# Layer boundaries of a graph network reordered on TensorE, a count scale applied at eviction, twelve tiles taken in row halves

## The chip, the cores and the metric

One core of one Trainium2 chip runs the whole program. The metric is the device time of one execution in microseconds (us). A kernel's time is the median of several executions without the profiler; the profile describes one further execution.

## What is computed

```python
# x: 6250 nodes x 128; src, dst: 200000 edges, sorted by dst; edge_weight per edge
z = x
for l in range(3):                                   # gated layers
    m   = z @ weight[l]
    agg = segment_sum(m[src] * edge_weight[:, None], dst)
    z   = gru_cell(agg, z, w_ih, w_hh, b_ih, b_hh)   # r, z gates: sigmoid; n: tanh; blend
x = layernorm(x + z)
y = x
for W, b in ((W0, b0), (W1, b1), (W2, b2)):          # count layers
    y = relu((y + segment_sum(y[src], dst)) @ W.T + b)
out = layernorm(x + y)
```

## The kernel before, in words

The nodes are padded to 6272, which is 49 tiles of 128. `xT` holds the features across the partitions and the nodes along the free dimension. The edge list is turned once into dense matrices in DRAM: `adj_w` (float32, sums of edge weights) and `adj_h` (float16, edge counts; the identity for the node's own term is part of it). A layer is then a dense product: for each of 14 groups of 448 target nodes, TensorE (PE) adds up 49 matmuls, one for each source tile, with the tile of `Y` (the layer's products, node-major) as the weights and a slab of the streamed matrix as the moving operand.

The program has four stages.

1. **Build, fused with the first gated layer.** 28 spans of 224 nodes. PE makes the matrix of a span out of one-hot operands (line 934, matmuls over 64 rows), and between the batches adds the 49 tiles of the span before (`add_tiles`, line 941). The last span has nothing left to build: its tiles 0 to 12, the gates of span 26, its tiles 13 to 48 and the gates of span 27 (`fused_gates`, lines 954 to 957) stand alone.
2. **Second gated layer**, `gru_layers(1, 1)`: `node_major` (line 719) makes the 49 products of the new layer, in chunks of four tiles that alternate between PSUM banks 6 and 7; DVE copies each chunk into `Y` (line 1300). Then `aggregate` (line 730) and `gates` (lines 740 to 743) for 14 groups, the gates of a group standing behind the aggregation of the next one.
3. **Third gated layer**, `last_gru_layer`: the same, with the sum with x, the statistics of the layer norm (`flip_sums`, line 819, and `statistics`) and, at its end, the products of the first count layer (`first_messages`, line 837), which ACT and DVE split into a high and a low float16 part (`first_highs`, line 1122; `first_lows`, line 1406).
4. **Three count layers**: `halves_of_group` (line 870) adds 49 tiles x 2 parts for each of 14 groups, `rectify` (line 1154) applies the relu. Between two of them stands `messages(l)`: a bound on the sums (line 845) gives a power-of-two scale, the weights are multiplied by it, transposed (line 847) and copied, and only then come the 49 products (line 853), split by ACT (line 1172) and DVE (line 1462).

Every fp32 matmul leaves two records in the trace, a float16 one leaves one. The queue of SyncE (SP) streams the matrix: four slabs of 12 or 13 tiles for each group in the gated layers (`ring`), two halves of 24 or 25 tiles for each group in the count layers (`ring_h`, two groups deep), each asked for when the slot that it fills has been used. All work is ordered by hand with semaphores: each engine runs its own list, and a wait holds up everything behind it on that engine.

The gates of group n wait for the blend of group n-1 (`s_gv`), since the mix of DVE reads banks 4 and 5 and the blend finishes `z`:

```python
pe.wait_ge(s_evac, FREE + n + 1)
pe.wait_ge(s_rz, START + 2 * n)
pe.wait_ge(s_gv, START + GV * n)
```

In the middle of a layer an aggregation stands between two gates and covers this. At the end of a layer nothing does, and `node_major` of the next layer waits for the last blend before its first product.

Of the kernel before, what the change touches and what calls it, by code (L numbers as in the profile page):

```python
# [39 lines left out]
SH = 13  # L40
HALF_TILES = [(0, 25), (25, 49)]
# [32 lines left out]
Y_BANKS = [0, 1, 6, 7] * 3 + [2, 3]  # L74
# [4 lines left out]
NC = len(CHUNKS)  # L79


def gnn_program(nc, x, src, dst, firsts, nodes, edges, edge_weight, gnn_w, w_ih, w_hh, b_ih, b_hh,
# [7 lines left out]
    with ctx:  # L90
# [54 lines left out]
        w_mean = averager[:, P - 1:P]  # L145
        row_averager = sb("row_averager", [P, GROUPS - 1 + P])
# [140 lines left out]
        s_fagg = sem("s_fagg")  # L287
        s_fev = sem("s_fev")
# [32 lines left out]
        SC = 9  # L321
        SC_FIRST = SC + 2
# [61 lines left out]
        AGG_BANK, COLUMN_BANK, RZ_BANK, IH_BANK = 4, 5, 6, 7  # L384
        agg_span = aggS[0][:, 0:SPAN]
# [27 lines left out]
        def _(sp):  # L413
# [56 lines left out]
            with sp.If(fits):  # L470
# [11 lines left out]
                for r in range(2):  # L482
                    for s in range(HALVES):

                        sp.wait_ge(s_used, SLABS * (N_LAYERS - 1) * GROUPS + HALVES * r + s + 1)
                        stream_counts(0, 0, r, s)
                for l in range(N_LAYERS - 1):
                    with sp.Fori(1 if l == 0 else 0, PAIRS) as i:
# [209 lines left out]
        def _(pe):  # L698
# [26 lines left out]
            def aggregate(n, bank, last=True):  # L725
                pe.wait_ge(s_evac, n + 1)
                for s, (h0, h1) in enumerate(SLAB_TILES):
                    pe.wait_ge(s_slab[s], 16 * (n + 1))
                    for h in range(h0, h1):
                        mm = pe.matmul(ps[:, bank, 0:GW], Y[:, h, :], ring[:, s, :, h - h0, :],  # L730
                                       start=(h == 0), stop=(last and h == TILES - 1))
                    mm.then_inc(s_used, 1)

            def gates(n, par, g):
# [3 lines left out]
                pe.wait_ge(s_gv, START + GV * n)  # L738
# [44 lines left out]

            def last_gru_layer():
# [18 lines left out]
                flip_sums(PAIRS - 2, (6, 7))  # L803
# [3 lines left out]
                first_messages(4, 8)  # L807
                flip_sums(PAIRS - 1, (4, 5))
                first_messages(8, 2 * PAIRS)

            def flip_sums(p, banks):

                pe.wait_ge(s_sum0, 2 * (p + 1))
                pe.wait_ge(s_norm0, START + PT * p)
                if p == 0:
                    pe.wait_ge(s_sc, SC_FIRST)
                for bank, (k0, k1) in zip(banks, PAIR_CHUNKS):
# [5 lines left out]
            def first_messages(lo, hi):  # L823
                for c in range(lo, hi):
# [9 lines left out]
                    elif bank >= 6:  # L834
                        pe.wait_ge(s_norm0, START + PT * (PAIRS - 1))
# [5 lines left out]
            def messages(l):  # L841
                pe.wait_ge(s_act, FREE + l * GROUPS)
                pe.wait_ge(s_norm0, START + TILES)
                pe.wait_ge(s_sc, sc_base(l) + 2)
                pe.matmul(ps[:, 2, 0:1], w_abs[:, :], x_top[:, :], start=True, stop=True).then_inc(s_bnd, 1)
                pe.wait_ge(s_sc, sc_base(l) + 7)
                pe.transpose(ps[:, 3, 0:P], w_row[:, :], ident[:, :]).then_inc(s_bnd, 1)
                pe.wait_ge(s_sc, sc_base(l) + 9)
                for j, (c, n) in enumerate(CHUNKS):

                    pe.wait_ge(s_ye1, START + y_base(l, TILES) + max(j - 3, 0))
                    for k in range(n):
                        mm = pe.matmul(ps[:, 4 + j % 4, k * P:(k + 1) * P], xT[:, tile_cols(c + k)], wcur[:, :],  # L853
                                       start=True, stop=True)
                    mm.then_inc(s_yp1, 1)

            def halves_of_group(l, i, par, parts, fresh=False):
                for s in parts:
                    h0, h1 = HALF_TILES[s]
                    pe.wait_ge(s_slab_h[HALVES * par + s], 16 * (PAIRS * l + i + 1))  # L860
                    for h in range(h0, h1):
                        if fresh and l == 0:
                            p, k = divmod(h, PT)
                            for c0, c1 in PAIR_CHUNKS:
                                if k == c0:
                                    pe.wait_ge(s_ye1, START + max(PT * p + c1, 4 * PT + 4))
# [21 lines left out]
            def count_layers():  # L888
                for l in range(N_LAYERS - 1):
                    if l:  # L890
                        messages(l)
                    for par in range(2):
# [53 lines left out]

            def fused_gates(n):
                xg = xT[:, bass.ds(n * SPAN, SPAN)]
                pe.wait_ge(s_fev, START + n + 1)
                pe.wait_ge(s_frz, START + 2 * n)  # L950
# [70 lines left out]
            add_tiles(0, SH, TILES)  # L1021
# [687 lines left out]
```

## Time and profile before

| | us |
|---|---|
| median of 3 executions | 3166.65 (3165.84 to 3167.36) |
| the profiled execution: its own time | 3150.35 |
| its span in the profile | 3148.6 |
| PE matmul busy | 3065.9 (97%) |
| DVE busy, ACT busy | 1124.0 (36%), 896.7 (28%) |
| mean granted clock of PE, share of full speed | 0.991 |
| the chain that ended last: share of PE | 97% |

The stages lie at 0 to 1080 us (build), 1080 to 1686 (second gated layer), 1686 to 2300 (third), 2300 to 3149 (count layers). The timeline view lists instructions of one engine merged into pieces: start, length, engine, line, shape and number of records, and in brackets how long the engine had been idle before the piece and what ended that. The length of a piece includes the modelled tail of its last matmul, so pieces on PE overlap a little.

### The profile page before, as it was taken

To read this page: it belongs to the slowest core of one execution; us is meant where nothing else is said; L and a number is where in the kernel's file an instruction comes from. 1 tells how busy PE (TensorE), PEld (TensorE's weight loads), DVE (VectorE), ACT (ScalarE), POOL (GpSimd) and SP (SyncE) were. 2 spreads that over 40 slices of the span, in tenths; PEclk is the share of its full clock that TensorE was granted. 3 is DMA by queue.
4 is the path that set the end of the run, shared out by engine and by line. 5 is a ranking of instruction groups with operands and counts; after the bars stand their busy time and mean duration, and the time that the engine had idled before them with its cause. 6 is when DMAs were issued, how large, how long until landed. Compare 5 with 4: busy or idle time off the path is not lost.

```text
span 3148.6 us, 74245 instructions
## 1 busy us (share of the span) xinstructions
PE 3065.9 (97%) x29934; PEld 1984.9 (63%) x29934; DVE 1124.0 (36%) x3088; ACT 896.7 (28%) x2099; POOL 291.1 (9%) x500
## 2 busy tenths in 40 slices
PE   5999999999999999999998999999989999999998
PEld 5888888888888855555555555555555555555554
DVE  5788888888888500000001011101130010001111
ACT  5666666666666300000000011110030010001111
POOL 3222232222222100000000000000000000000000
PEclk9999999999999999999999999999999999999999
DMA  5555655655655686767674766677647867785884
GB/s 188 226 243 222 256 240 226 256 236 228 254 236 231 260 314 264 278 264 276 266 311 165 288 263 268 266 286 275 263 176 295 311 253 285 295 311 224 308 311 167
DMA packets 135446, 809.63 MB, mean 257 GB/s; under 512 B 7972, under 2 KB 17432, under 8 KB 120776
## 3 DMA queue, kind: packets, MB, share of 16 engines
q1 hardware_dynamic: 129704, 800.52, 65.0%
q0 software_dynamic: 4368, 7.97, 0.9%
q8 instruction: 59, 0.97, 0.1%
q10 hardware_dynamic: 1296, 0.01, 0.0%
q14 instruction: 19, 0.16, 0.0%
HBM read 566.04 MB, written 242.44 MB: 257 GB/s over the span
## 4 chain that ended last, share of the span: by engine, by line
PE 97%; DVE 1%; issue 1%; ACT 1%; DMA 0%; POOL 0%; DVEq 0%; ACTq 0%; POOLq 0%
PE ps L730 33%; PE ps L870 25%; PE ps L941 19%; PE ps L934 11%; PE ps L740 1%; PE ps L741 1%; PE ps L719 1%; PE ps L853 1%; PE ps L954 1%; PE ps L955 1%; PE ps L743 1%; PE ps L742 1%; PE ps L1000 0%; PE ps L957 0%; PE ps L956 0%
## 5 line engine op out<-in xcount | busy, mean ns | idle before, releaser
L730 PE MATMUL ps<-ring,Y 128*128 128x448 f32 x2744 | 1035.7, 539 | 1.9 <-DVE Y L1300 1.9
L730 PEld LDWEIGHTS ps<-ring,Y 128*128 128x128 f32 x2744 | 521.2, 190 | 511.4 <-issue 511.4
L870 PE MATMUL ps<-ring,Y 128*128 128x448 f16 x4116 | 781.9, 353 | 2.1 <-DVE Y L1406 2.1
L1240 ACT ACTIVATE ring<-ps 128x392 f16<-128x392 f32 (+1 forms) x1568 | 654.8, 507 | 285.4 <-PE ps L934 280.4
L870 PEld LDWEIGHTS ps<-ring,Y 128*128 128x128 f16 x4116 | 403.2, 98 | 377.6 <-issue 3.9
L941 PE MATMUL ps<-ring,Y 128*128 (+1 forms) x2744 | 614.7, 366 | 0.4 <-ACT shared L1202 0.4
L941 PEld LDWEIGHTS ps<-ring,Y 128*128 128x128 f32 x2744 | 491.3, 190 | 15.4 <-ACT shared L1202 0.8
L934 PEld LDWEIGHTS ps<-shared 64*128 64x128 bf16 x18816 | 334.6, 94 | 115.0 <-ACT ring L1240 86.7
L1575 DVE TENSOR_TENSOR shared<-shared 128x400 bf16<-128x400 bf16 x1176 | 396.3, 390 | 0.0
L934 PE MATMUL ps<-shared 64*128 64x49 bf16 (+1 forms) x18816 | 378.3, 190 | 10.7 <-issue 9.4
L1071 ACT ACTIVATE shared<-ps 128x448 f32<-128x448 f32 x28 | 15.2, 543 | 984.9 <-PE ps L730 984.9
L1308 DVE SCALAR_TENSOR_TENSOR shared<-ps,bhh,shared 128x448 f32<-128x448 f32 x28 | 19.1, 684 | 740.7 <-ACT shared L1076 740.7
L1571 DVE TENSOR_TENSOR shared<-iota_lo,shared 128x1024 bf16<-128x1024 bf16 x392 | 278.3, 710 | 0.0
L1154 ACT ACTIVATE xT<-ps,bcur,unscale 128x448 f32 (+1 forms) x42 | 30.4, 723 | 701.5 <-PE ps L870 701.5
L1469 DVE TENSOR_REDUCE x_tops<-xT x28 | 17.4, 620 | 501.5 <-ACT xT L1154 501.5
L1569 DVE TENSOR_TENSOR shared<-iota_key,shared 128x400 bf16<-128x400 bf16 x392 | 147.9, 377 | 114.0 <-PE ps L934 101.7
L611 POOL DMA_INDIRECT shared<-in_edges,take_now x60 | 60.4, 1007 | 371.3 <-PE ps L934 368.4
L1437 DVE TENSOR_TENSOR shared<-shared,ps 128x384 f32 (+3 forms) x14 | 8.7, 621 | 228.7 <-PE ps L885 228.4
L1383 DVE BATCH_NORM_STATS2 averager<-ps 128x6 f32<-128x128 f32 x49 | 10.4, 281 | 192.8 <-PE ps L819 192.8
L740 PE MATMUL ps<-shared,wT 128*128 128x448 f32 x112 | 53.4, 560 | 9.4 <-DVE xT L1319 9.4
L741 PE MATMUL ps<-xT,wT 128*128 128x448 f32 (+1 forms) x112 | 52.9, 555 | 0.0
L636 POOL CAST shared<-shared 128x224 bf16<-128x224 f32 x87 | 44.3, 510 | 14.6 <-POOL shared L638 9.7
(149 smaller groups left out, 1249.9 us busy)
## 6 DMA issues: line engine op xcount, KB each, us to landing
ring<-adj_w SPq DMA_DIRECT2D x84, 2688.0 KB, 8.9
adj_w<-ring SPq DMA_DIRECT2D x56, 2744.0 KB, 12.3
ring<-adj_h SPq DMA_DIRECT2D x42, 2800.0 KB, 9.4
ring<-adj_h SPq DMA_DIRECT2D x42, 2688.0 KB, 9.1
ring<-adj_w SPq DMA_DIRECT2D x28, 2912.0 KB, 9.4
adj_h<-ring SPq DMA_DIRECT2D x56, 1372.0 KB, 5.0
x_keep<-xT SPq DMA_DIRECT2D x1, 3136.0 KB, 10.8
shared<-x_keep SPq DMA_DIRECT2D x1, 3136.0 KB, 15.7
```

Source lines behind the costliest of these rows:

```text
L611: pool.indirect_dma_start(out=edges_now[:, par, d * SHARE:d * SHARE + OWN, :].bitcast(I32) .rearrange("p e k -> p (e k)"), out_offset=None ...
L636: col_step(pool.tensor_copy(part, twice(rest).to_broadcast([P, 1, LANES, 2])))
L730: mm = pe.matmul(ps[:, bank, 0:GW], Y[:, h, :], ring[:, s, :, h - h0, :], start=(h == 0), stop=(last and h == TILES - 1))
L740: pe.matmul(ps[:, bank, 0:GW], wT[:, c, :], aggS[par], start=True, stop=False)
L741: pe.matmul(ps[:, bank, 0:GW], wT[:, 3 + c, :], xg, start=False, stop=True)
L870: mm = pe.matmul(ps[:, par, 0:GW], part[:, h, :], ring_h[:, par, s, :, h - h0, :], start=(h == 0 and part is Y_high), stop=(h == TILES - 1 ...
L934: mm = pe.matmul(sums, hot_lo[slots, buf, w, :], rhs, start=(part == 0), stop=(part == WPARTS - 1))
L941: mm = pe.matmul(ps[:, AGG_BANK, 0:SPAN], Y[:, h, :], strip_w[:, bass.ds(slot, 1), :, h, :].rearrange("p o b c -> p (o b) c"), start=(h == ...
L1240: act.activation(strip[:, :, c0:c0 + UNIT * WIN].rearrange("p h (d j) -> p d h j", d=WIN), psum_unit(a)[:, :, kind, :, :].rearrange("p d j ...
L1569: dve.tensor_tensor(in_pairs(hot[:, buf, :, 0, :]), every_window(iota_key, WIDE), values(par, 0, k, WIDE), ALU.is_equal).then_inc(s_hot, 1)
L1571: dve.tensor_tensor(in_pairs(hot_lo[:, buf, :, :]), every_window(iota_lo, P), values(par, 1, k, P), ALU.is_equal).then_inc(s_hot, 1)
L1575: dve.tensor_tensor(in_pairs(hot[:, buf, :, 1 + part, :]), in_pairs(hot[:, buf, :, 0, :]), values(par, 2 + part, k, WIDE), ALU.mult).then_ ...
```

## The change

Line numbers of the changed kernel differ: `node_chunks` is line 746, `aggregate` 758, `gates` 768 to 771, `flip_sums` 870, `first_messages` 892, `messages` 903 and 908, `halves_of_group` 924, `add_tiles` 1003, `add_halves` 1014, `fused_gates` 1029 to 1032.

- The 49 products of the second and third gated layer are cut into chunks (`node_chunks`) that stand around and between the last gates of the layer before, each chunk waiting for no more of `xT` than it reads. They rotate through three or four banks, and ACT in place of DVE copies them into `Y`. The aggregation waits chunk by chunk.
- In the unrolled places, `gates` waits for two of the five DVE steps of the group before (the mix), no longer for the whole blend.
- At the end of the third layer the flips of pairs 5 and 6, their statistics and the last first messages move behind the gates and between the halves of the first two count groups; those four halves run in the order (group 0, first), (group 1, first), (group 0, second), (group 1, second), and SP asks for the next ones in that order.
- Between count layers the weights are no longer scaled: the products run on the unscaled weights into six banks from the start, and the scale is applied by ACT and DVE when they empty the banks. The bound comes from one matmul after the second chunk; the transpose and the copy of the weights are gone.
- Tiles 37 to 48 of the last span run as two matmuls of 64 rows each, into banks 4 and 0, and DVE adds the two banks' results before the gates.

```diff
-Y_BANKS = [0, 1, 6, 7] * 3 + [2, 3]
+Y_BANKS = [0, 1, 6, 7, 0, 1, 6, 7, 2, 3, 2, 3, 4, 5]
+WHOLE_ROWS = 37
+SECOND_BANKS = [1, 2, 3, 5] * 3 + [1]
+THIRD_BANKS = [6, 7, 0] * 3 + [6, 7, 6, 7]
...
+            def node_chunks(layer, lo, hi, banks):
+                for j in range(lo, hi):
+                    c, n = CHUNKS[j]
+                    users = [i for i in range(j) if banks[i] == banks[j]]
+                    if users:
+                        pe.wait_ge(s_ye, START + NC * (layer - 1) + users[-1] + 1)
+                    if layer == 1:
+                        pe.wait_ge(s_fgv, START + GV * min(((c + n) * P - 1) // SPAN + 1, GATHERS))
+                    else:
+                        pe.wait_ge(s_gv, START + GV * (((c + n) * P - 1) // GW + 1))
+                    for k in range(n):
+                        mm = pe.matmul(ps[:, banks[j], k * P:(k + 1) * P], xT[:, tile_cols(c + k)], gw[:, layer, :],
+                                       start=True, stop=True)
+                    mm.then_inc(s_yp, 1)
...
             def gates(n, par, g):
-                pe.wait_ge(s_gv, START + GV * n)
+                pe.wait_ge(s_gv, START + GV * (n - 1) + 2 if isinstance(n, int) else START + GV * n)
...
+            def second_gru_layer():
+                node_chunks(1, 0, 3, SECOND_BANKS)
+                fused_gates(GATHERS - 1)
+                node_chunks(1, 3, NC, SECOND_BANKS)
+                aggregate(0, 0, chunks_of=1)
...
+                aggregate(GROUPS - 1, 1)
+                gates(GROUPS - 2, 0, GROUPS - 2)
...
             def last_gru_layer():
-                pe.wait_ge(s_gv, START + GV * n0)
-                node_major(1, gw[:, N_LAYERS - 1, :])
-                aggregate(n0, 0)
+                node_chunks(2, 0, first, THIRD_BANKS)
+                gates(GROUPS - 1, 1, GROUPS - 1)
+                node_chunks(2, first, first + 1, THIRD_BANKS)
+                aggregate(n0, 0, slabs=range(2), chunks_of=2, ...)
+                node_chunks(2, first + 1, NC, THIRD_BANKS)
+                aggregate(n0, 0, slabs=range(2, SLABS), chunks_of=2)
...
                 aggregate(n0 + GROUPS - 1, 1)
-                flip_sums(PAIRS - 2, (6, 7))
                 gates(n0 + GROUPS - 2, 0, GROUPS - 2)
                 first_messages(0, 4)
                 gates(n0 + GROUPS - 1, 1, GROUPS - 1)
-                first_messages(4, 8)
-                flip_sums(PAIRS - 1, (4, 5))
-                first_messages(8, 2 * PAIRS)
+                first_messages(4, 10)
+                flip_sums(PAIRS - 2, (4, 5))
...
             def messages(l):
-                pe.wait_ge(s_act, FREE + l * GROUPS)
-                pe.wait_ge(s_sc, sc_base(l) + 2)
-                pe.matmul(ps[:, 2, 0:1], w_abs[:, :], x_top[:, :], start=True, stop=True).then_inc(s_bnd, 1)
-                pe.wait_ge(s_sc, sc_base(l) + 7)
-                pe.transpose(ps[:, 3, 0:P], w_row[:, :], ident[:, :]).then_inc(s_bnd, 1)
-                pe.wait_ge(s_sc, sc_base(l) + 9)
                 for j, (c, n) in enumerate(CHUNKS):
+                    if j >= 6:
+                        pe.wait_ge(s_ye1, START + y_base(l, TILES) + j - 5)
+                    pe.wait_ge(s_act, FREE + (l - 1) * GROUPS + ((c + n) * P - 1) // GW + 1)
                     for k in range(n):
-                        mm = pe.matmul(ps[:, 4 + j % 4, k * P:(k + 1) * P], xT[:, tile_cols(c + k)], wcur[:, :],
+                        mm = pe.matmul(ps[:, 2 + j % 6, k * P:(k + 1) * P], xT[:, tile_cols(c + k)],
+                                       wT[:, 2 * N_LAYERS + l, :], start=True, stop=True)
+                    if j == 1:
+                        pe.wait_ge(s_sc, sc_base(l) + 3)
+                        pe.matmul(ps[:, 0, 0:1], w_top[:, :].to_broadcast([P, P]), x_top[:, :], ...)
...
             def count_layers():
+                    else:
+                        halves_of_group(0, 0, 0, (0,), fresh=True)
+                        flip_sums(PAIRS - 1, (6, 7))
+                        first_messages(10, 12)
+                        halves_of_group(0, 0, 1, (0,), fresh=True)
+                        first_messages(12, 14)
+                        for par in range(2):
+                            halves_of_group(0, 0, par, (1,), fresh=True)
...
+            def add_halves(slot, lo, hi):
+                for h in range(lo, hi):
+                    for r, bank in enumerate((AGG_BANK, HALF_BANK)):
+                        rows = slice(r * P // 2, (r + 1) * P // 2)
+                        mm = pe.matmul(ps[:, bank, 0:SPAN], Y[rows, h, :], strip_w[rows, slot, :, h, :],
+                                       start=(r == 1 and h == lo), stop=(h == TILES - 1))
...
-            add_tiles(0, SH, TILES)
+            add_tiles(0, SH, WHOLE_ROWS)
+            add_halves(0, WHOLE_ROWS, TILES)
...
# ACT, between count layers
-                                           ps[:, 4 + j % 4, ...], ACT.Copy)
+                                           ps[:, 2 + j % 6, ...], ACT.Copy, scale=scale[:, 0:1].bitcast(F32))
# DVE, between count layers
-                            dve.tensor_tensor(Y_low[:, c:c + n, :], ps[:, 4 + j % 4, ...], Y_high[...], ALU.subtract)
+                            dve.scalar_tensor_tensor(out=Y_low[:, c:c + n, :], in0=ps[:, 2 + j % 6, ...],
+                                                     scalar=scale[:, 0:1].bitcast(F32), in1=Y_high[...],
+                                                     op0=ALU.mult, op1=ALU.subtract)
# DVE, last span
+            dve.wait_ge(s_fev, START + GATHERS)
+            dve.tensor_tensor(by_unit(agg_span), by_unit(agg_span), natural(ps[:, HALF_BANK, 0:SPAN]), ALU.add)
```

Three places of PE's list show the moves. The first is the end of the second gated layer, from its last aggregation on, in the kernel before (719 are the products, 730 the aggregation, 740 to 743 the gates):

```order
L730 MATMUL ps<-ring,Y 128x448 x49
L740 MATMUL ps<-shared,wT 128x448
L741 MATMUL ps<-xT,wT 128x448
L740 MATMUL ps<-shared,wT 128x448
L741 MATMUL ps<-xT,wT 128x448
L742 MATMUL ps<-shared,wT 128x448
L743 MATMUL ps<-xT,wT 128x448
L740 MATMUL ps<-shared,wT 128x448
L741 MATMUL ps<-xT,wT 128x448
L740 MATMUL ps<-shared,wT 128x448
L741 MATMUL ps<-xT,wT 128x448
L742 MATMUL ps<-shared,wT 128x448
```

There the gates of the last two groups follow each other, and all 49 products stand behind them. The same place in the changed kernel (746 products, 758 aggregation, 768 to 771 gates), from the last gate matmul of group 12 on:

```order
L771 MATMUL ps<-xT,wT 128x448
L746 MATMUL ps<-gw,xT 128x128 x40
L768 MATMUL ps<-shared,wT 128x448
L769 MATMUL ps<-xT,wT 128x448
L768 MATMUL ps<-shared,wT 128x448
L769 MATMUL ps<-xT,wT 128x448
L770 MATMUL ps<-shared,wT 128x448
L771 MATMUL ps<-xT,wT 128x448
L746 MATMUL ps<-gw,xT 128x128 x4
L758 MATMUL ps<-ring,Y 128x448 x25
L746 MATMUL ps<-gw,xT 128x128 x5
L758 MATMUL ps<-ring,Y 128x448 x73
```

Forty products have moved between the two sets of gates, and the last five stand inside the next aggregation. The second place is PE's list around the second count layer's products in the changed kernel:

```order
L903 MATMUL ps<-wT,xT 128x128 x8
L908 MATMUL ps<-x_top,averager 128x1
L903 MATMUL ps<-wT,xT 128x128 x41
L924 MATMUL ps<-ring,Y 128x448 x196
```

Before, the bound (845) and the transpose (847) stood ahead of all 49 products (853); now eight products stand ahead of the bound, and there is no transpose. The third place is the end of the last span in the changed kernel:

```order
L1003 MATMUL ps<-ring,Y 128x224 x24
L1014 MATMUL ps<-ring,Y 128x224 x24
L1099 TENSOR_LOAD flag
L1099 ISA x2
L1100 COMPARE_AND_BRANCH
L746 MATMUL ps<-gw,xT 128x128 x12
L1029 MATMUL ps<-shared,wT 128x224
```

Where 36 matmuls of 128 rows stood (line 941), 24 such and 24 of 64 rows stand, and the branch and twelve products now come ahead of the gates of span 27.

## Rows read from the trace of the kernel before

**Rows 1.** The page, busy time: engine, busy us (share), instructions
```profile
PE 3065.9 (97%) x29934; PEld 1984.9 (63%) x29934; DVE 1124.0 (36%) x3088; ACT 896.7 (28%) x2099; POOL 291.1 (9%) x500
```
**Rows 2.** Waits of PE over the span: total us, times, longest us
```profile
PE ps L740 <- DVE xT L1319: 9.4, 2, 5.0
```
**Rows 3.** Timeline of PE and DVE, last span and start of the second gated layer
```profile
1065.39 13.89 PE L941 MATMUL ps<-ring,Y 128*128 128x224 f32 x72
...
1085.13 0.39 DVE L1550 TENSOR_TENSOR xT<-xT,shared 128x224 f32<-128x224 f32 x1
...
1085.89 13.58 PE L719 MATMUL ps<-gw,xT 128*128 128x128 f32 x98 [3.63 <-DVE xT L1550]
1100.42 5.88 PE L730 MATMUL ps<-ring,Y 128*128 128x448 f32 x15 [0.94 <-DVE Y L1300]
```
**Rows 4.** Timeline of PE, second to third gated layer
```profile
1670.26 0.92 PE L740 MATMUL ps<-shared,wT 128*128 128x448 f32 x2
...
1674.02 0.92 PE L743 MATMUL ps<-xT,wT 128*128 128x448 f32 x2
...
1679.98 1.67 PE L740 MATMUL ps<-shared,wT 128*128 128x448 f32 x2 [5.04 <-DVE xT L1319]
...
1691.37 14.60 PE L719 MATMUL ps<-gw,xT 128*128 128x128 f32 x98 [4.95 <-DVE xT L1319]
1706.97 21.29 PE L730 MATMUL ps<-ring,Y 128*128 128x448 f32 x56 [1.00 <-DVE Y L1300]
```
**Rows 5.** Timeline of PE, third gated layer to first count layer
```profile
2280.98 0.93 PE L819 MATMUL ps<-ident,xT 128*128 128x128 f32 x7
...
2293.87 1.17 PE L740 MATMUL ps<-shared,wT 128*128 128x448 f32 x2 [4.33 <-DVE xT L1319]
...
2305.82 0.98 PE L819 MATMUL ps<-ident,xT 128*128 128x128 f32 x7 [2.38 <-DVE xT L1397]
...
2314.17 11.11 PE L870 MATMUL ps<-ring,Y 128*128 128x448 f16 x49 [2.12 <-DVE Y L1406]
```
**Rows 6.** Timeline of PE, from one count layer to the next, both times
```profile
2569.71 5.84 PE L870 MATMUL ps<-ring,Y 128*128 128x448 f16 x30
...
2593.72 6.60 PE L870 MATMUL ps<-ring,Y 128*128 128x448 f16 x34
...
2849.66 3.76 PE L870 MATMUL ps<-ring,Y 128*128 128x448 f16 x19
...
2872.37 9.81 PE L870 MATMUL ps<-ring,Y 128*128 128x448 f16 x51
```
**Rows 7.** Stretches: window, us, PE busy (records), PEld busy, ..., granted clock, DMA share, GB/s
```profile
2580.00:2582.00 2.00, 1.36 (x6) 1.14 (x6) 0.44 (x2) 0.00 (x0) 0.00 (x0) 0.50 1.02 425
2350.00:2550.00 200.00, 200.00 (x1059) 103.43 (x1058) 6.82 (x11) 7.96 (x11) 0.00 (x0) 1.00 0.80 301
```
**Rows 8.** Stretch of line 853 alone: PE busy, PEld busy, granted clock, DMA share, GB/s
```profile
2585.00:2593.00 8.00, 8.00 (x74) 8.00 (x73) 1.00 0.00 0
```
**Rows 9.** Timeline of DVE behind the gates of group 12, second layer
```profile
1676.36 0.68 DVE L1311 SCALAR_TENSOR_TENSOR shared<-ps,bih,shared 128x448 f32<-128x448 f32 x1
...
1679.20 0.62 DVE L1319 TENSOR_TENSOR xT<-xT,shared 128x448 f32 x1
```
**Rows 10.** Instructions by shape: evictions of products; busy us, mean ns | idle before
```profile
L1172 ACT ACTIVATE Y<-ps 128x512 f16<-128x512 f32 x24 | 14.3, 597 | 22.2 <-PE ps L853 22.2
...
L1220 ACT ACTIVATE Y<-ps 128x512 f32<-128x512 f32 x12 | 8.4, 699 | 2.4 <-PE ps L1000 2.4
```
**Rows 11.** Timeline of PE in the build: 64-row records and 128-row records in turn
```profile
1052.18 0.95 PE L934 MATMUL ps<-shared 64*128 64x98 bf16 x48
1053.07 1.78 PE L941 MATMUL ps<-ring,Y 128*128 x8
1054.78 0.95 PE L934 MATMUL ps<-shared 64*128 64x98 bf16 x48
```
**Rows 12.** DMA issues at 1080 to 1110 us: count, KB each, median us to landing
```profile
ring<-adj_w SPq DMA_DIRECT2D x3, 2688.0 KB, 22.5
```

More of the change, by code:

```diff
@@ L1077, in update, with tanh, take_chunks @@
                 act.activation(z_t, ps[:, 3, 0:GW], ACT.Sigmoid, bias=brz[:, 1:2]).then_inc(s_rz, 1)
+            def tanh(n):
                 act.wait_ge(s_gv, START + GV * n + 2)
                 act.activation(n_t, t_t, ACT.Tanh).then_inc(s_n, 1)
+            def update(n):
+                sigmoids(n)
+                tanh(n)
+            def take_chunks(layer, lo, hi, banks):
+                for j in range(lo, hi):
+                    c, n = CHUNKS[j]
+                    act.wait_ge(s_yp, NC * (layer - 1) + j + 1)
+                    act.activation(Y[:, c:c + n, :], ps[:, banks[j], 0:n * P].rearrange("p (c f) -> p c f", f=P), ACT.Copy)\
+                       .then_inc(s_ye, 1)
             def gru_layers(first, layers):
@@ L1123, in first_highs, with second_gru_layer @@
                                        scale=scales[:, t:t + 1]).then_inc(s_yh, 1)
+            def second_gru_layer():
+                take_chunks(1, 0, 3, SECOND_BANKS)
+                fused_sigmoids(GATHERS - 1)
+                take_chunks(1, 3, 4, SECOND_BANKS)
+                fused_tanh(GATHERS - 1)
+                take_chunks(1, 4, NC, SECOND_BANKS)
+                evac(0, 0)
+                with act.Fori(0, PAIRS - 1) as i:
+                    evac(2 * i + 1, 1)
+                    update(2 * i)
+                    evac(2 * i + 2, 0)
+                    update(2 * i + 1)
+                evac(GROUPS - 1, 1)
+                sigmoids(GROUPS - 2)
+                take_chunks(2, 0, 2, THIRD_BANKS)
+                tanh(GROUPS - 2)
             def last_gru_layer():
                 n0 = GROUPS
+                first = len([j for j, (c, n) in enumerate(CHUNKS) if (c + n) * P <= (GROUPS - 2) * GW])
+                take_chunks(2, 2, first, THIRD_BANKS)
+                sigmoids(GROUPS - 1)
+                take_chunks(2, first, first + 1, THIRD_BANKS)
+                tanh(GROUPS - 1)
+                take_chunks(2, first + 1, NC, THIRD_BANKS)
                 evac(n0, 0)
@@ L1319, in gru_group @@
                 dve.tensor_tensor(xg, xg, n_t, ALU.add).then_inc(s_gv, 1)
+            def gru_group(n, g):
+                mix(n)
+                blend(n, g)
             def gru_layers(first, layers):
@@ L1394, in sum_group, with blend_and_sum @@
             def sum_group(n, g):
-                gru_group(n, g)
+                mix(n)
+                blend_and_sum(n, g)
+            def blend_and_sum(n, g):
+                blend(n, g)
                 dve.wait_ge(s_gv, START + GV * (n + 1))
@@ L1613, in _ @@
             with dve.If(fits):
-                gru_layers(1, 1)
+                with dve.Fori(0, GROUPS) as g:
+                    gru_group(g, g)
+                dve.wait_ge(s_gv, START + GV * GROUPS)
                 last_gru_layer()
```

193 lines of the change are left out of this document (125 added, 68 removed).

## The prediction

> **What bounds the kernel now.** The page comes first: PE is busy for 97% of the span [rows 1], and no other engine for more than 36%. So only two things can be won: PE's idle time, and time in which PE works slowly or on work that can be dropped. Next the waits of PE. The largest that the change touches is the gates' wait for the blend of the group before, 9.4 us in two places [rows 2]; the others stand in brackets in the timeline rows of the five layer boundaries [rows 3 to 5]. At a boundary the reader is to see one pattern: gates, an idle time while ACT and DVE finish the group, more gates or products, idle again. Inside the layers no such gap stands: 200 us of a count layer hold 200.00 us of matmul [rows 7].
>
> Idle time is not all. The stretches view shows a granted clock of 0.50, the 1.2 GHz level, right behind the gap between two count layers, and 1.00, the 2.4 GHz level, inside the layers [rows 7]. The timeline says the same: six gate matmuls of two records have a pitch of (1674.02 - 1670.26) / 5 = 0.752 us at full clock, while the piece that follows the gap of 5.04 us is 1.67 long in place of 0.92 [rows 4]. So each boundary costs its gaps and a slow stretch behind them. I price a boundary as a whole: from the end of the work before it to the first matmul of the next aggregation, less the work in between at full clock.
>
> Prices at full clock: a set of gates over 448 columns 6 x 0.752 = 4.51 us [rows 4]. Products: 74 records start in 8.00 us of dense work [rows 8], 0.108 us each, or 0.11 with the edges of the window; 49 products are 98 records, 10.8 us. Transposes of a pair: 0.76 us (2280.98 to the gates at 2281.74; the row's 0.93 has a tail) [rows 5].
>
> **The boundaries, one by one.**
>
> *Build to second gated layer.* From the last tile's end, 1065.39 + 13.89 = 1079.28, to the aggregation at 1100.42 are 21.1 us [rows 3]. The work in it is 10.8 plus the gates over 224 columns, 12 records at the 0.193 us that 72 such records show (13.89 / 72), 2.3: together 13.1. In the changed order twelve products (2.7 us) cover ACT's eviction, DVE's new addition (0.4 to 0.5 us, the kind of operation that takes 0.62 over 448 columns [rows 9]) and its semaphores, and 32 of the other 37 products (7.0 us) cover the last blend, which now takes some 3.6 us [rows 3]. New on the path is the branch that used to stand in the idle time. No row isolates it; the first product came 0.4 us after the blend had ended at 1085.52 [rows 3], so I take 0.4, between 0 (PE's list runs ahead) and 1.5 (the load of the flag waits too). Gain 21.1 - 13.5 = 7.6.
>
> *Second to third gated layer.* 1670.26 to 1706.97 are 36.7 us [rows 4]. Work: two sets of gates and 49 products, 9.0 + 10.8 = 19.8. The wait of the second gates becomes one for the mix, which ended at 1676.36 + 0.68 = 1677.04, 2.8 us before the blend's end at 1679.82 [rows 9]; 40 products (8.8 us) stand in front of it, so either is covered. Three banks rotate. ACT needs 0.70 us for a chunk [rows 10], PE 8 x 0.11 = 0.88, so ACT keeps up, and its sigmoids and tanh (0.6 us each) cost it at most a chunk of lead. The last five products wait for the last blend behind 25 tiles of aggregation, 50 records or 19 us. Gain 36.7 - 19.8 = 16.9.
>
> *Third gated layer to the counts.* 2280.98 to 2314.17 are 33.2 us [rows 5]. Work: two sets of gates 9.0, two sets of flips 1.5, 49 products 10.8: 21.3. Behind it the first 49 count records took 11.11 us, where 1059 records in 200 us make 0.189 each [rows 5, 7], 9.3: another 1.8 of slow clock. In the changed order fourteen products (3.1 us) stand before the last gates, which need the mix, some 2.3 us after the first gates; the last statistics run while PE adds two half groups of 50 records, 9.4 us each. DVE and ACT have in this stretch the same highs and lows as before, some 3.7 us for 14 tiles, and the counts need 18 lows to begin with, all of pairs 0 and 1 and part of 2. I find them 2 us early. Gain 33.2 - 21.3 + 1.8 = 13.7.
>
> *Count to count, twice.* 2575.55 to 2593.72 are 18.2 us, and 2853.42 to 2872.37 are 19.0 [rows 6]. The changed work is 10.8 plus the bound. Two chunks (1.8 us) stand ahead of it; the relu, the maximum and its reduction need about 2.1, so 0.3 of waiting remains, and the matmul itself I put at 0.3. Transpose, scaled weights and their copy vanish. The scale is known some 1.5 us after the bound; six banks hold 5.3 us of products meanwhile, and the evictions (0.6 on ACT [rows 10], 0.7 to 0.8 on DVE) are faster than PE's 0.88. Gain 18.2 - 11.4 = 6.8 and 19.0 - 11.4 = 7.6.
>
> **The row halves.** 24 records of 128 rows become 48 of 64 rows. The 64-row records of the build show that two halves do work at once: 48 of them, of 49 and 98 columns, 3136 columns in all, have a pitch of 0.88 us [rows 11], while one after another at 2.4 GHz they would need 1.31. But fp32 halves stand in no row. Abreast, 24 pairs cost what 24 whole records cost, 4.6 us, and nothing is won, since each half streams all 224 columns; one after another they cost 4.6 more. The nearest row is the one of 64-row records, so I take them abreast, plus two switches between the shapes: eight whole records between two batches take 1.71 us where 8 x 0.193 is 1.54 [rows 11, 3], 0.17 for each, 0.3 for both. Ends: 0.2 below nothing (a record's 0.193 less its 448 cycles of 0.187) and 5.0 above.
>
> The Trainium skill (TensorE: Matmul & The Clock Gate, What overlaps and what doesn't) says that a weight load overlaps a running matmul only where the row groups differ. By it the whole records would pay for their loads and the halves would save them. The trace disagrees for whole records: 72 in 13.89 us is the streaming time alone. By that rule the halves would bring a gain, by the row none. Against the halves stands TensorEngine Tiling (Array Packing), Key Properties, also of the Trainium skill: a change of tiling mode drains the engine; the 0.17 us agree.
>
> **The sum.** 7.6 + 16.9 + 13.7 + 6.8 + 7.6 = 52.6, less 0.3 for the halves: 52.3. I keep 2.3 back for hand-overs between short pieces, which each had a few hundredths here: 50. The profiled execution took 3150.35 and would take 3100; the median is 16.3 above that one, a difference which the change has no part in, so 3166.65 - 50 = 3116.6, rounded 3117. The gaps in brackets in rows 3 to 5 are 24.4 of it; the rest is the gaps between the count layers, the slow clock behind all of them, and chunks paced by two banks.
>
> **Rivals.**
>
> 1. *Halves one after another* (PE's order, or loads that share a path): 4.6 more, 3122. For it: fp32 weights have no 64-row row here. Against it: rows 11. Chance 0.2.
> 2. *A gap comes back.* ACT is now in every chain between the last gates: evictions stand between sigmoids and tanh. Should PE outrun it at one or two boundaries, a gap of 2.4 us and its slow stretch (1.7 us, half of some 3.4) return, 4 to 8 us: 3121 to 3125, and with the first rival up to 3130. Against it: ACT's 0.70 against 0.88. Chance 0.13.
> 3. *The halves gain*, by the skill's rule above in this kernel's terms: loads of the two groups side by side, 24 pairs at 0.11 in place of 0.193, 2 us less, 3115. Whole records already run at their streaming time, so 0.04.
> 4. *Slower than before*: the matrix stream. PE takes a half group in 9.4 us and the stream already moves 301 GB/s [rows 7]. SP asks in the new order once, and (group 1, first) is asked for a half later. Four requests at once took 22.5 us to land [rows 12]; a slot is needed 28 us after it is free, 19 us for this one. If the order left the stream behind for good, each of some 80 halves would have to come 0.65 us late to eat 52 us, which decides at a stream below some 280 GB/s. Against it: 425 GB/s in rows 7. Then 3168 or more. Chance 0.01.
> 5. *The reordering is there but its stretches are not faster*: the slow clock stays without gaps, because products of 128 columns are thin work. Half of the gain would go: 3141. Against it: rows 8, full clock over 8 us of exactly such work. Chance 0.03.
>
> The forecast itself has 0.58, with 3111 to 3121 as its own range: the 2.3 us kept back may not be needed, or be three times as much. The range of 3109 to 3131 holds it, the first three rivals and what they give together. A measurement can tell 0.2%, 6 us, from no change; all cases but the fourth are beyond it: faster 0.98, slower 0.01, and 0.01 within for what none of them names.
>
> **What would show it.** Right: no idle above 0.5 us on PE between the layers, save the one before the bound; a granted clock of 1.00 through all five boundaries; 98 product records of a boundary in about 10.8 us; the aggregation of the second gated layer about 14 us behind the last tile. The halves are right if their 48 records take 4.6 to 5 us, wrong at 9. The forecast is wrong if gates wait for DVE in the changed boundaries, if count matmuls wait for DMA, or if PE's chunks stand behind ACT's evictions.

## The result

| | before | changed |
|---|---|---|
| median of the executions, us | 3166.68 | 3115.57 |
| lowest to highest (4 each) | 3165.84 to 3167.36 | 3113.49 to 3116.77 |
| span of the profiled execution, us | 3148.6 | 3114.7 |
| mean granted clock | 0.991 | 0.997 |

The ratio is 0.9838, with a 95% interval of 0.9821 to 0.9855: 51.1 us faster. The forecast was 3117, 50 us faster. The median lies 1.4 us below it. The profiled execution of before (3150.35 us) is not among its four; the experiments show why it is 16 us shorter than they are.

### The profile page after: what moved, and what is told of

The parts are those of the page before. It is cut to its first block, busy times and chain, and to the rows that moved or that the text cites. A ratio compares the mean times of both kernels' runs of the same rounds, so it can differ in the third digit from the quotient of the medians.

```text
span 3114.7 us, 74296 instructions
## 1 busy us (share of the span) xinstructions
PE 3055.5 (98%) x29956; PEld 1975.7 (63%) x29956; DVE 1107.2 (36%) x3061; ACT 909.9 (29%) x2123; POOL 291.1 (9%) x500
## 4 chain that ended last, share of the span: by engine, by line
PE 98%; issue 1%; DMA 0%; DVE 0%; ACT 0%; POOL 0%; DVEq 0%; POOLq 0%; ACTq 0%
PE ps L758 33%; PE ps L924 25%; PE ps L1003 19%; PE ps L996 11%; PE ps L768 1%; PE ps L769 1%; PE ps L1029 1%; PE ps L746 1%; PE ps L1030 1%; PE ps L771 1%; PE ps L770 1%; PE ps L903 1%; PE ps L1075 0%; PE ps L892 0%; PE ps L1031 0%
## 5 line engine op out<-in xcount | busy, mean ns | idle before, releaser
L996 PE MATMUL ps<-shared 64*128 64x49 bf16 (+1 forms) x18816 | 386.7, 190 | 19.3 <-issue 16.3
L1611 DVE TENSOR_REDUCE x_tops<-xT x28 | 17.4, 620 | 482.3 <-ACT xT L1274 482.3
L1514 DVE BATCH_NORM_STATS2 averager<-ps 128x6 f32<-128x128 f32 x49 | 10.4, 281 | 162.2 <-PE ps L870 160.8
L768 PE MATMUL ps<-shared,wT 128*128 128x448 f32 x112 | 51.3, 540 | 0.0
```

What stands on the lines that cost most here:

```text
L768: pe.matmul(ps[:, bank, 0:GW], wT[:, c, :], aggS[par], start=True, stop=False)
L996: mm = pe.matmul(sums, hot_lo[slots, buf, w, :], rhs, start=(part == 0), stop=(part == WPARTS - 1))
```

## The profile after

The head of the page: PE's share rose from 97% to 98% and its busy time fell by 10.4 us. Against a second profile of before, taken below and like this one in its build stage, it fell by 20.8 us (3076.3 to 3055.5).

```profile
span 3114.7 us, 74296 instructions
PE 3055.5 (98%) x29956; PEld 1975.7 (63%) x29956; DVE 1107.2 (36%) x3061; ACT 909.9 (29%) x2123; POOL 291.1 (9%) x500
```

The waits of PE (total us, times, longest). The gates' wait of [rows 2] is gone, and of all waits at the boundaries only the one before the bound (908) is left:

```profile
PE ps L996 <- issue: 16.3, 31, 2.9
...
PE ps L908 <- DVE x_top L1487: 1.3, 2, 0.7
```

The timeline of PE where the build ends (1003 whole tiles, 1014 halves, 746 products, 758 aggregation), which answers to [rows 3]:

```profile
1082.42 9.35 PE L1003 MATMUL ps<-ring,Y 128*128 128x224 f32 x48
1091.70 4.81 PE L1014 MATMUL ps<-ring,Y 64*128 64x224 f32 x48
1096.44 2.94 PE L746 MATMUL ps<-gw,xT 128*128 128x128 f32 x24
...
1101.50 8.42 PE L746 MATMUL ps<-gw,xT 128*128 128x128 f32 x74
1109.76 0.54 PE L758 MATMUL ps<-ring,Y 128*128 128x448 f32 x1
```

From the second to the third gated layer, against [rows 4]. No row has a bracket:

```profile
1679.52 0.91 PE L768 MATMUL ps<-shared,wT 128*128 128x448 f32 x2
...
1684.03 9.09 PE L746 MATMUL ps<-gw,xT 128*128 128x128 f32 x80
...
1698.37 18.96 PE L758 MATMUL ps<-ring,Y 128*128 128x448 f32 x50
1717.16 1.28 PE L746 MATMUL ps<-gw,xT 128*128 128x128 f32 x10
1718.28 27.23 PE L758 MATMUL ps<-ring,Y 128*128 128x448 f32 x72
```

From the third gated layer to the counts, against [rows 5] (892 first messages, 870 flips, 924 counts):

```profile
2273.42 0.91 PE L768 MATMUL ps<-shared,wT 128*128 128x448 f32 x2
...
2277.93 3.29 PE L892 MATMUL ps<-late,xT 128*128 128x128 f32 x28
...
2291.02 9.62 PE L924 MATMUL ps<-ring,Y 128*128 128x448 f16 x50
2300.47 0.93 PE L870 MATMUL ps<-ident,xT 128*128 128x128 f32 x7
2301.24 1.73 PE L892 MATMUL ps<-late,xT 128*128 128x128 f32 x14
2302.80 9.62 PE L924 MATMUL ps<-ring,Y 128*128 128x448 f16 x50
2312.26 1.72 PE L892 MATMUL ps<-late,xT 128*128 128x128 f32 x14
2313.82 26.46 PE L924 MATMUL ps<-ring,Y 128*128 128x448 f16 x139
```

Between count layers, against [rows 6]; the second one has the same lengths from 2826.08 to 2838.18:

```profile
2554.44 1.95 PE L903 MATMUL ps<-wT,xT 128*128 128x128 f32 x16
2557.06 0.38 PE L908 MATMUL ps<-x_top,averager 128*128 128x1 f32 x2 [0.67 <-DVE x_top L1487]
2557.30 9.40 PE L903 MATMUL ps<-wT,xT 128*128 128x128 f32 x82
2566.54 33.65 PE L924 MATMUL ps<-ring,Y 128*128 128x448 f16 x177
```

Two stretches of products in the changed kernel, one at the second to third gated layer and one between count layers (length, then busy time and records of each engine; third from the end is the granted clock):

```profile
1684.00:1692.00 8.00, 8.00 (x73) 7.96 (x72) 3.25 (x5) 6.18 (x11) 0.00 (x0) 1.00 0.50 210
2558.00:2566.00 8.00, 8.00 (x74) 8.00 (x74) 7.14 (x13) 6.81 (x11) 0.00 (x0) 1.00 0.66 272
```

Boundary by boundary, measured as the prediction did, in us (the first row includes the last tiles; lengths run from the first to the last time given):

| boundary | before | changed | gain | forecast |
|---|---|---|---|---|
| build to second gated (1065.39 to 1100.42; 1082.42 to 1109.76) | 35.0 | 27.3 | 7.7 | 7.6 - 0.3 |
| second to third gated (changed: 1679.52 to 1698.37, and 1.1 inside the aggregation) | 36.7 | 20.0 | 16.7 | 16.9 |
| third gated to counts (changed: 17.6 to the first half, then 2.3 and 1.6), with the slow start of the counts | 33.2 + 1.8 | 21.5 | 13.5 | 13.7 |
| first to second count | 18.2 | 12.1 | 6.1 | 6.8 |
| second to third count | 19.0 | 12.1 | 6.9 | 7.6 |
| sum | | | 50.9 | 52.3, less 2.3 kept back |

The two profiled spans differ by 33.9 us only, 17.0 less than this sum. That piece lies wholly in the build stage, which the change does not touch: the last span's first lone tiles (those with no building beside them) start at 1057.89 in the first profile and at 1074.92 here. So a doubt was open: had the change slowed the build?

## The experiments

**The kernel before, profiled again.** No edit.

> The kernel before, unchanged, profiled once more. Its first profiled execution took 3150.35 us, its other executions 3166 to 3167; the changed kernel's profile has the same length as its other executions, and its build stage (up to the last span's first lone tile) ends at 1074.92 us in place of 1057.89. Theory: the first profile of before caught an unusually quick build stage, the usual one is about 17 us longer, with some 30 idle pieces of PE put down to issue; then this profile shows the lone tiles starting near 1075 and a span near 3165. Rival: the build stage of before is always the quick one and the 16 us lie outside the profiled span; then it starts near 1058 again, and the changed kernel has made the build stage 17 us slower by itself.

Its median was 3167.85, ratio 1.0003 (0.9994 to 1.0013). The span of this profile is 3166.0 us, and the lone tiles start at 1075.63. The stretch from 500 to 600 us, first of the earlier profile of before, then of this one (us, PE busy and records, and so on):

```profile
500.00:600.00 100.00, 100.00 (x2170) 87.77 (x2170) 88.69 (x246) 68.38 (x168) 28.68 (x47) 1.00 0.59 242
```

The same stretch in the second profile:

```profile
500.00:600.00 100.00, 99.25 (x2123) 86.77 (x2123) 87.18 (x241) 66.82 (x164) 28.69 (x47) 1.00 0.57 233
```

2% fewer matmul records for the same program at the same clock. One trip of the build's inner loop (one span of 224 nodes) takes 36.26 us in the first profile and 36.86 in this one, and 26 such trips make most of the 17 us. The build stage has two lengths, and the change has no part in it. Against this profile the changed span is 51.3 us shorter, as the sum by boundaries says.

**Whole tiles in place of halves.**

```diff
-            add_tiles(0, SH, WHOLE_ROWS)
-            add_halves(0, WHOLE_ROWS, TILES)
+            add_tiles(0, SH, TILES)
...
-            dve.tensor_tensor(by_unit(agg_span), by_unit(agg_span), natural(ps[:, HALF_BANK, 0:SPAN]), ALU.add)
```

> The changed kernel with tiles 37 to 48 of the last span as whole matmuls again, without DVE's addition. Theory (halves run abreast): the 24 records take 4.6 us where the 48 halves took 4.74, the time changes by 0.1 to 0.4 us, which only the timeline can show. Rival (the halves gain or cost something at the hand-over to the products): the first product starts over 1 us sooner or later behind the last tile.

3116.18 in the one execution. The tiles and the first products:

```profile
1082.34 13.89 PE L1003 MATMUL ps<-ring,Y 128*128 128x224 f32 x72
1096.07 2.84 PE L746 MATMUL ps<-gw,xT 128*128 128x128 f32 x24
```

13.73 us from the first tile to the first product, 14.02 in the changed kernel: 0.3 us less, as expected. The total of one execution can't show so little.

**All 36 lone tiles in halves.**

```diff
-WHOLE_ROWS = 37
+WHOLE_ROWS = 13
```

> The changed kernel with all 36 lone tiles of the last span in halves in place of 12. Theory (abreast, one price per change of shape): 144 half records take 3 x 4.7 = 14.2 us, against 13.9 for 72 whole ones. Rival (each half has its own overhead, hidden in 12 tiles by the records queued ahead): clearly over 15 us, up to 27.8 if one after another.

3118.12 in the one execution, and the same two rows:

```profile
1084.16 13.89 PE L1014 MATMUL ps<-ring,Y 64*128 64x224 f32 x144
1097.98 2.94 PE L746 MATMUL ps<-gw,xT 128*128 128x128 f32 x24
```

144 half records take the time of 72 whole ones, 13.82 us. The group of their weight loads (busy time, then mean ns of one) says that the halves work at the same time:

```profile
L1014 PEld LDWEIGHTS ps<-ring,Y 64*128 64x128 f32 x144 | 13.5, 187 | 0.0
```

144 loads of 187 ns each would fill 26.9 us one after another, and they fill 13.5: two fp32 halves in two banks run abreast. The row halves are worth nothing and cost nothing but 0.1 to 0.3 us where shapes change. The 2 us of the total lie before these tiles, which start 1.7 us later than in the changed kernel, in the build stage.

**The gates wait for the blend again.**

```diff
-                pe.wait_ge(s_gv, START + GV * (n - 1) + 2 if isinstance(n, int) else START + GV * n)
+                pe.wait_ge(s_gv, START + GV * n)
```

> The changed kernel with one wait put back: gates wait for the whole blend of the group before, not for its mix. Theory: between the second and third gated layer 40 products (8.9 us) cover it, no gap; before the last gates of the third layer only 14 products (3.1 us) stand, and the blend ends 5 to 5.6 us behind the first gates, so a gap of 2 to 2.5 us, with or without a slow stretch of 1.7 us behind it: 2 to 4 us slower, 3118 to 3120. Rival (the order alone does it, the relaxed wait is idle): no gap, same time. Second rival: the gates inside the third layer start to wait too, over 10 us.

3120.17 (3118.31 to 3121.24), ratio 0.9849 (0.9833 to 0.9866). One wait appeared, before the last gates of the third layer:

```profile
2285.69 0.99 PE L768 MATMUL ps<-shared,wT 128*128 128x448 f32 x2 [2.26 <-DVE xT L1447]
```

From the first gates to the first half count it took 20.1 us in place of 17.6, 2.5 more. Forty products do cover the wait at the other boundary, where no wait appeared, fourteen do not; the granted clock stayed at 1.00, the 2.4 GHz level, behind this gap. The other 2 us or so of the 4.6 lie in the build stage: the lone tiles start at 1077.13 in place of 1074.92, and the last gates but one are late by the same 2.2 us.

**The scale on the weights again.** One part undone, between the count layers only.

```diff
             def messages(l):
+                pe.wait_ge(s_act, FREE + l * GROUPS)
+                pe.wait_ge(s_sc, sc_base(l) + 2)
+                pe.matmul(ps[:, 2, 0:1], w_abs[:, :], x_top[:, :], ...)
+                pe.wait_ge(s_sc, sc_base(l) + 7)
+                pe.transpose(ps[:, 3, 0:P], w_row[:, :], ident[:, :])
+                pe.wait_ge(s_sc, sc_base(l) + 9)
...
-                        mm = pe.matmul(ps[:, 2 + j % 6, ...], xT[:, tile_cols(c + k)], wT[:, 2 * N_LAYERS + l, :], ...)
+                        mm = pe.matmul(ps[:, 4 + j % 4, ...], xT[:, tile_cols(c + k)], wcur[:, :], ...)
```

> The changed kernel with one part undone: between the count layers the bound, the scaled and transposed weights and their copy stand ahead of the products again, four banks, no scale at eviction. The traces give the two boundaries 12.1 us each now, 18.2 and 19.0 before. Theory (parts add up): 13 us slower, 3128 to 3129, with the gaps of 2.4, 1.2 and 0.6 us and the slow clock back. Rival (the eviction with a scale is what costs, and only the early start gains): under 10 us. Second rival (the gain came from six banks in place of four): the products alone would pace at over 0.11 us a record at full clock.

This set of runs met the quick build: before took 3149.77 in it. The sets ran on different chips (the one so far on chip 10, this one on chip 0, the last one below on chip 2), so the length may belong to the chip as well as to the set; for the very first profiles no chip is on record. This kernel took 3110.73, ratio 0.9876 (0.9859 to 0.9892). The second of its two boundaries:

```profile
2811.72 3.38 PE L925 MATMUL ps<-ring,Y 128*128 128x448 f16 x17
2817.53 0.35 PE L900 MATMUL ps<-x_top,late 128*128 128x1 f32 x2 [2.43 <-DVE x_top L1487]
2819.10 0.33 PE L902 MATMUL ps<-ident,late 128*128 128x128 f32 x1 [1.21 <-DVE late L1599]
2820.07 12.56 PE L908 MATMUL ps<-late,xT 128*128 128x128 f32 x98 [0.64 <-DVE bcur L1602]
2832.46 23.81 PE L925 MATMUL ps<-ring,Y 128*128 128x448 f16 x125
```

The boundaries took 18.2 and 17.4 us, 11.4 more than the changed kernel's 2 x 12.1: 1.6 under the 13 that was expected, and over the 10 of the first rival. Both times the three gaps are 4.3 us, and the 98 records of products take 12.9 and 12.4 us in place of some 11, by the slow stretch. Behind that stretch four banks are enough: 20 records start in each 2 us from 2547 to 2555 us, and 20 or 21 in the changed kernel with its six, so the second rival is out. In the changed kernel the 82 records (41 products) after the bound keep 0.113 us a record (9.24 / 82), so the scaled eviction costs PE nothing.

**A gap put in on purpose.**

```diff
-                        pe.wait_ge(s_gv, START + GV * (((c + n) * P - 1) // GW + 1))
+                        pe.wait_ge(s_gv, START + GV * max(((c + n) * P - 1) // GW + 1, GROUPS - 1))
...
-                take_chunks(2, 0, 2, THIRD_BANKS)
                 tanh(GROUPS - 2)
+                take_chunks(2, 0, 2, THIRD_BANKS)
```

> The changed kernel with one gap put in on purpose: between the second and third gated layer the first products wait for the last but one blend (ACT takes tanh ahead of the evictions, so that the blend can end). Nothing else moves, so this prices a gap by itself. Theory (gap plus slow stretch behind it): a gap of 4.8 to 4.9 us, then a granted clock of 0.50 for a stretch of 3.4 us, or two of them, 1.7 us lost in each: 6.5 to 8.5 us slower, 3122 to 3124. Rival (the slow clock before came from several gaps in a row, one alone does not bring it): 4.9 us, 3120 to 3121.

3105.68 beside 3149.77 for before. The changed kernel was not run in this set; by the 50.9 us of the control below it would be at 3098.9, so 6.8 slower. The timeline says it without that detour, with the idle time and what ended it in the bracket:

```profile
1673.33 11.45 PE L746 MATMUL ps<-gw,xT 128*128 128x128 f32 x80 [4.95 <-DVE xT L1447]
```

Two stretches behind that gap:

```profile
1675.00:1677.00 2.00, 2.00 (x11) 2.00 (x11) 0.00 (x0) 0.60 (x1) 0.00 (x0) 0.50 0.00 0
1679.00:1681.00 2.00, 2.00 (x20) 2.00 (x20) 0.00 (x0) 1.35 (x3) 0.00 (x0) 1.00 0.00 0
```

Eleven records of products in 2 us at 0.50, the 1.2 GHz level, and twenty at 1.00, the 2.4 GHz level. The 80 records (40 products) took 11.3 us to the next gates in place of 8.9. From the first gates to the aggregation it took 26.3 us (1663.71 to 1690.02) in place of 18.9: a gap of 5 us costs 7.4, and the rival without a slow stretch is out.

**The second boundary undone**: both sets of gates one after the other, the full waits, all products behind the last blend.

```diff
-                pe.wait_ge(s_gv, START + GV * (n - 1) + 2 if isinstance(n, int) else START + GV * n)
+                pe.wait_ge(s_gv, START + GV * n)
...
+                gates(GROUPS - 1, 1, GROUPS - 1)
+                pe.wait_ge(s_gv, START + GV * GROUPS)
                 node_chunks(2, 0, first, THIRD_BANKS)
-                gates(GROUPS - 1, 1, GROUPS - 1)
                 node_chunks(2, first, first + 1, THIRD_BANKS)
...
# ACT
-                take_chunks(2, 2, first, THIRD_BANKS)
                 sigmoids(GROUPS - 1)
-                take_chunks(2, first, first + 1, THIRD_BANKS)
                 tanh(GROUPS - 1)
-                take_chunks(2, first + 1, NC, THIRD_BANKS)
+                take_chunks(2, 0, NC, THIRD_BANKS)
```

> The changed kernel with the order between the second and third gated layer undone: both sets of gates follow each other, gates wait for the whole blend, and all products wait for the last one. Three banks, ACT's evictions and the chunk-wise start of the aggregation stay. Theory: two gaps of 4.9 to 5.0 us come back, with slow stretches behind both (1.7 us on the gates, 1.7 to 3.4 on the products): 13.5 to 15 us; the waits cost 2.5 us more before the last gates of the third layer, as in the run with that wait alone. 16 to 17.5 us slower than the changed kernel beside it. Rival (most of this boundary's 16.7 us came from banks and chunk-wise waits, not from the order): under 12 us.

3132.62 beside 3115.43 for the changed kernel: 17.2 slower. Its rows:

```profile
1678.95 0.92 PE L768 MATMUL ps<-shared,wT 128*128 128x448 f32 x2
...
1688.67 1.83 PE L768 MATMUL ps<-shared,wT 128*128 128x448 f32 x2 [5.05 <-DVE xT L1445]
...
1701.40 11.72 PE L746 MATMUL ps<-gw,xT 128*128 128x128 f32 x88 [4.96 <-DVE xT L1445]
1712.95 17.45 PE L758 MATMUL ps<-ring,Y 128*128 128x448 f32 x46
...
2298.05 0.99 PE L768 MATMUL ps<-shared,wT 128*128 128x448 f32 x2 [2.25 <-DVE xT L1445]
2298.88 1.65 PE L769 MATMUL ps<-xT,wT 128*128 128x448 f32 x2
```

34.0 us from the first gates to the aggregation in place of 18.9, 15.1 more: of this boundary's 16.7 us the order with its waits makes 15, which leaves 1.6 for banks and chunk-wise waits. Before the last gates of the third layer the gap of 2.25 us had a slow stretch behind it this time (1.65 us for a piece of 0.92), which the gap of 2.26 us above had not.

**The control.** The changed kernel once more, in the set of the run above.

> The changed kernel, unchanged, once more, as the control for the runs beside it. In the first runs of this study before took 3167 to 3168 and its profile showed 32 idle pieces of PE put down to issue in the build; in the second set before took 3150 and the profiles of that set's kernels with the single-span loop body showed 6. Theory: the build stage has two lengths, 17 us apart, that stay the same through one set of runs, and the change has no part in it: the difference to before is 50 to 52 us in either case (3098 to 3100 if before takes 3150, 3115 to 3117 if it takes 3167). Rival (the change helps less with the quick build): under 48.

3115.43 beside 3166.31 for before: 50.9 us, ratio 0.984 (0.9826 to 0.9853). With the long build, then, the gain is 51 us twice. In the quick set the changed kernel itself was not run; the version that follows was run in both kinds of set, and stays 52.5 and 52.1 us under before.

**A version past the change.** The bound after the third chunk, whole tiles; twice, once in each kind of set.

```diff
-                    if j == 1:
+                    if j == 2:
                         pe.wait_ge(s_sc, sc_base(l) + 3)
...
-            add_tiles(0, SH, WHOLE_ROWS)
-            add_halves(0, WHOLE_ROWS, TILES)
+            add_tiles(0, SH, TILES)
```

> The changed kernel with two edits: the bound's matmul stands behind the third chunk in place of the second, and the last twelve tiles are whole. Theory: PE's wait of 0.67 us before the bound goes, twice, and 0.3 us of the halves: 1.6 us faster, 3114, and the evictions that start 0.3 us later are still ahead of PE. Rival (the later scale makes PE wait for a bank at the seventh chunk): no gain or up to 1 us slower.

3097.24 beside 3149.77 for before, ratio 0.9833 (0.9817 to 0.9849): 52.5 us under before.

> The kernel with the bound after the third chunk and whole last tiles, beside the changed kernel on the same chip. Theory: 1.6 us faster than it (twice 0.67 us of waiting and 0.3 us of the halves); the spans differ by that, the medians by 1 to 2.5. Rival: no difference.

3114.23 beside 3115.43 for the changed kernel: 1.2 us faster, spans 3114.2 and 3115.3. Both ranges overlap, so the gain rests on the timeline, where the wait is gone and the boundary is 11.2 us long in place of 12.1:

```profile
2555.65 2.84 PE L903 MATMUL ps<-wT,xT 128*128 128x128 f32 x24
2558.32 0.32 PE L908 MATMUL ps<-x_top,averager 128*128 128x1 f32 x2
...
2566.86 13.40 PE L924 MATMUL ps<-ring,Y 128*128 128x448 f16 x70
```

**The build loop written out.**

```diff
-                with pe.Fori(0, 2) as slot:
+                for slot in range(2):
                     build_span(2 * i + slot + 2, slot, 2 * i + slot)
```

> The changed kernel with PE's inner build loop (two slots, one body) written out, so that one trip of the outer loop holds two spans. In the usual build stage PE loses about 0.3 us at two places of every trip of the inner loop, always the same places, put down to issue; the one quick profile did not. Theory A (the stall belongs to the jump back at a trip's end, which now comes half as often): about 8 us faster, 3107, one pair of stalls for two spans. Theory B (it belongs to the run of instructions, so many per block): two stalls for each span as now, same time, perhaps at other places.

3159.31, slower than before in the same set (ratio 1.0033, 1.002 to 1.0045), some 60 us above the changed kernel's 3098.9 worked out above. Both theories fell. Its waits:

```profile
PE ps L996 <- issue: 46.3, 41, 2.9
...
PE ps L1003 <- issue: 6.4, 13, 0.5
```

Its instruction queue (packets, MB, share):

```profile
q8 instruction: 234, 3.83, 0.5%
```

In the other profiles of the changed kernel and its variants the first of these is 9.6 to 16.5 us. That queue moved 59 packets in the kernel before and 60 in the changed one. PE waits for issue more often, and the instruction queue moves four times the packets. That a body of two spans is fetched again on each trip, and a body of one is not, would fit both; no run here separates it.

## Why the prediction was right

**The price of a boundary** held. Taking each one whole, as its length less the work at full clock, gave 52.3 against 50.9 measured. A sum of the gaps alone would have given 33; the gap put in on purpose shows why, 5 us of idle cost 7.4. The 2.3 us kept back were meant for hand-overs between short pieces. What they covered was 1.4 us, nearly all of it the count boundaries below; that the two are of one size is luck.

**The halves** were right in kind and size: abreast, nothing won, 0.1 to 0.3 us for the changes of shape. The first and the third rival are out: 144 halves took 13.82 us, 72 whole records 13.73. The two changes of shape together cost at most 0.3 us. The rule of the Trainium skill (TensorE: Matmul & The Clock Gate, What overlaps and what doesn't) is that a load overlaps a running matmul only where the row groups differ. For the halves the trace agrees, their loads overlap; for whole records it disagrees, since their loads of 190 ns leave the pitch at 0.191 us (13.73 / 72), and so the halves had nothing to save.

**The cover** was right where it was counted: 40 products hide a blend, 14 hide a mix, and 14 do not hide a blend (2.26 us of waiting with the old wait). The second rival did not come: PE waits for an ACT eviction at no boundary.

**The count boundaries** were the terms most off, 6.8 and 7.6 against 6.1 and 6.9. The step was the wait before the bound, put at 0.3 us and measured at 0.67. DVE makes the magnitudes and their maximum (0.2 and 0.3 us) behind the last group's maximum (1611) and not ahead of it, and the bound's wait ends with the last of these rows:

```profile
2556.27 0.22 DVE L1483 TENSOR_SCALAR late<-wT 128x128 int32<-128x128 int32 x1
2556.52 0.29 DVE L1596 TENSOR_REDUCE averager<-late 128x1 f32<-128x128 f32 x1
2556.84 0.17 DVE L1487 TENSOR_REDUCE x_top<-x_tops 128x1 f32<-128x14 f32 x1
```

Products cost 0.112 us a record, not 0.11: 0.2 us for each boundary.

**The branch** was put at 0.4 us. From the end of the halves to the aggregation stand 13.3 us, of which 13.2 are the gates and products at their pace, so it costs 0.1 at most. That fits the lower end of the prediction, PE's list running ahead of its work; no run separates it.

**The slow clock** went with the gaps: the granted clock is 1.00, the 2.4 GHz level, in the changed kernel's stretches from 1082 to 1110, 1679 to 1720, 2273 to 2315, 2554 to 2568 and 2826 to 2840 us, so the fifth rival is out. The stream kept up, with no wait of PE for DMA: the fourth is out.

**The 16.3 us** between the profiled execution and the median were carried over as if outside the matter. That gave the right total by luck: they were the build stage's two lengths, and the executions behind both medians happened to have the same one. The profiled execution, forecast at 3100, took 3116.43, and comparing the two spans would have shown 33.9 us in place of 51.

## What to carry to other kernels

Where PE is busy for 97%, price each stage boundary as a whole, its length less its work at full clock; the slow clock behind a gap made a 5 us gap cost 7.4. Independent work of the next stage belongs between the last dependent pieces of this one, and each wait should name the step that frees the operand (the mix), not the end of the group (the blend). A common factor that is known late can be applied when results leave PSUM; PE then starts without it.

## What the runs showed of the hardware

- The same program has a build stage of two lengths, 17 us apart (before: medians of 3149.77 in one set of runs, 3166.3 to 3167.9 in the others). In the longer one PE pauses at two fixed places of each span, which make a trip 0.4 and 0.2 us longer; where the view shows a bracket it says issue, that is, nothing in the profile ended the pause. What decides between the lengths stays open: each later set ran on a chip of its own. Within a set it did not change, save for the very first profile of before.
- Writing the loop out made it 60 us slower, with four times the instruction packets.
- Two fp32 matmuls of 64 rows, 224 columns, in two banks cost what one of 128 rows costs: 0.096 us for each half record against 0.191.
- A gap of 2.25 us was once followed by the 1.2 GHz level and once not.
